# Query stage of a four-layer token kernel: where two routed blocks are located, and the order inside GpSimd's inverse root

## The reference, cut to what matters

```python
q_p = elu(einsum('bhnd,hdf->bhnf', q, proj)) + 1.0
attn = einsum('bhnf,bhfd->bhnd', q_p, kv) * z
x = x + attn.reshape(b, n, d) @ W_out.T + b_out
xt = layernorm(x)
logits = xt @ w_g                      # 8 experts, the top 2 are taken
exp_rank = cumsum(one_hot(top_i)) - 1  # a token's slot in its expert's list
exp_mask = exp_mask * (exp_rank < cap)
```

## Time and profile before

| what | us |
|---|---|
| median of 3 runs | 519.93 |
| the runs | 519.93, 519.01, 523.59 |
| the profiled execution's own time | 518.94 |
| its span | 517.2 |

### The profile page before, as it was taken

The page is one execution under the profiler, slowest core; times in us unless marked ns, Lnnn a source line. Parts: engine busy times, 40 slices in busy tenths (PEclk is TensorE's granted clock), DMA queues, the critical chain, the costliest instruction groups (busy, mean ns, idle before and its releaser), DMA issues.

```text
span 517.2 us, 7944 instructions
## 1 busy us (share of the span) xinstructions
PE 447.1 (86%) x2774; PEld 312.4 (60%) x2774; DVE 295.3 (57%) x712; ACT 228.7 (44%) x351; POOL 257.3 (50%) x321
## 2 busy tenths in 40 slices
PE   7889797968578999999999999889776989999980
PEld 5534253425578788888876333335355977887860
DVE  5879789998230021424486999899775201221254
ACT  5758554433020333324047998877652113323220
POOL 5989575898535945455431000021715542555460
PEclk9989777879778999999999999999978799999995
DMA  5465742991198222125423443340101121221277
GB/s 133 144 227 162 253 136 89 333 270 39 42 285 264 74 74 60 53 77 190 150 59 94 101 102 95 89 160 1 38 15 37 42 88 35 60 81 54 63 226 210
DMA packets 50327, 60.87 MB, mean 118 GB/s; under 512 B 7152, under 2 KB 29296, under 8 KB 50288
## 3 DMA queue, kind: packets, MB, share of 16 engines
q1 hardware_dynamic: 42672, 47.50, 31.1%
q0 software_dynamic: 4608, 8.47, 5.0%
q10 hardware_dynamic: 3008, 4.40, 2.7%
HBM read 29.78 MB, written 25.31 MB: 107 GB/s over the span
## 4 chain that ended last, share of the span: by engine, by line
PE 36%; issue 20%; SPq 12%; DVE 4%; DMA 3%; another core or an unknown queue 2%; ACT 1%; POOLq 0%; POOL 0%; ACTq 0%; DVEq 0%
PE ps L1342 29%; SPq L391 11%; PE ps L1346 5%; PE ps L1498 2%; DMA last_got<-chosen_y 1%; DMA slots_x<-rows_x,put_at 1%; DMA xe<-slots_x 1%; DMA chosen_y<-ye,y_to 0%; DMA stk<-part 0%; ACT xnT L586 0%; DVE xeT L1177 0%; POOLq L81 0%; DVE otok L997 0%; DVE xn L1237 0%
## 5 line engine op out<-in xcount | busy, mean ns | idle before, releaser
L543 POOL DMA_INDIRECT chosen_y<-ye,y_to x80 | 79.1, 988 | 78.0 <-DVE ye L1212 54.1
L493 POOL DMA_INDIRECT slots_x<-rows_x,put_at x64 | 62.7, 980 | 48.8 <-DVE put_at L1071 31.6
L1346 PE MATMUL ps<-ident 128*128 128x128 f32 x584 | 78.8, 298 | 6.4 <-DMA slots_x<-rows_x,put_at 3.2
L719 ACT ACTIVATE hT<-ps 128x640 f32<-128x640 f32 x64 | 45.1, 704 | 87.2 <-issue 49.5
L1346 PEld LDWEIGHTS ps<-ident 128*128 128x128 f32 x584 | 74.2, 156 | 9.1 <-DMA slots_x<-rows_x,put_at 3.9
L1266 DVE SCALAR_TENSOR_TENSOR feat<-expo,ps 128x1024 f32<-128x1024 f32 x64 | 76.4, 1217 | 2.4 <-ACT expo L848 2.0
L848 ACT ACTIVATE expo<-ps,minus_one 128x1024 f32<-128x1024 f32 x64 | 70.4, 1116 | 12.8 <-PE ps L1342 8.9
L1342 PE MATMUL ps<-cproj_sb,hT 128*128 128x128 f32 x640 | 74.6, 275 | 0.3
L1342 PEld LDWEIGHTS ps<-cproj_sb,hT 128*128 128x128 f32 x640 | 73.0, 192 | 0.9 <-issue 0.6
L1342 PE MATMUL ps<-xeT,cfc_sb 128*128 128x320 f32 x256 | 71.7, 433 | 2.1 <-DVE xeT L1177 2.1
L1177 DVE COPY xeT<-ps 128x640 f32<-128x640 f32 x16 | 13.2, 825 | 94.5 <-PE ps L1342 47.3
(11 more groups left out here) (230 smaller groups left out, 612.9 us busy)
## 6 DMA issues: line engine op xcount, KB each, us to landing
chosen_y<-empty_rows SPq DMA_DIRECT2D x32, 256.0 KB
decay<-k_rows SPq DMA_DIRECT2D x30, 256.0 KB, 4.8
stk<-part SPq DMA_DIRECT2D x96, 64.0 KB, 2.0
slots_x<-empty_rows SPq DMA_DIRECT2D x16, 325.0 KB, 5.7
xe<-slots_x SPq DMA_DIRECT2D x16, 325.0 KB
cfc_sb<-in_L_ffn_c_fc SPq DMA_DIRECT2D x2, 2048.0 KB, 9.1
got<-chosen_y SPq DMA_DIRECT2D x8, 256.0 KB
got<-chosen_y ACTq DMA_DIRECT2D x8, 256.0 KB
```

Of the source, the lines that this page charges most:

```text
L493: pool.indirect_dma_start(out=slots_x[k], out_offset=bass.IndirectOffsetOnAxis(ap=put_at[:, c, kk, t:t + 1], axis=0), in_=rows_x[:, kk * N ...
L543: pool.indirect_dma_start(out=chosen_y[k], out_offset=bass.IndirectOffsetOnAxis(ap=y_to[:, b, i:i + 1], axis=0), in_=ye[:, b, i * D:(i + 1 ...
L719: act.activation(hT[:, b, f, :].rearrange("p (a n) -> p a n", a=2), ps[:, 2 + 2 * (f % 2):4 + 2 * (f % 2), 0:HALF], ACT.Gelu).then_inc(h_r ...
L1346: pe.transpose(ps[:, bank, 0:P], ident[:], ident[:])
```

## The change

The rank slots of blocks 0 and 1 come one unit earlier: block 0 is located in slot 25, between units 5 and 6 of block 2, and block 1 in slot 36, between units 5 and 6 of block 3. Unit 6 moves to slots 26 and 37. All the rest keeps its slot. In `inverse_root`, `half` is computed right after `var_eps`, and the negated mean right after that, straight into `shift`; both without a link. The number of instructions on each engine is the same.

```diff
 def unit_slot(c, u):
-    return 8 * c + u + max(0, c - 1) + 2 * max(0, c - 2) + (u > 4) * (c >= 1) + ((u > 3) + (u > 6)) * (c >= 2)
+    return 8 * c + u + max(0, c - 1) + 2 * max(0, c - 2) + (u > 4) * (c >= 1) + ((u > 3) + (u > 5)) * (c >= 2)
...
-RANK_AT = {unit_slot(c + 2, 6) + 1: c for c in range(NB - 2)}
+RANK_AT = {unit_slot(c + 2, 5) + 1: c for c in range(NB - 2)}
...
                 link_root(pool.tensor_scalar(var_eps[:], mv[:, tt, 1], EPS, None, ALU.add))
+                pool.tensor_scalar(half[:], var_eps[:], 0.5, None, ALU.mult)
+                pool.tensor_scalar(shift[:, tt], mv[:, tt, 0], -1.0, None, ALU.mult)
                 link_root(pool.tensor_scalar(guess[:].bitcast(I32), var_eps[:].bitcast(I32), -0.5, float(0x5F3759DF),
                                              ALU.mult, ALU.add))
-                link_root(pool.tensor_scalar(half[:], var_eps[:], 0.5, None, ALU.mult))
                 y = guess[:]
                 for it in range(3):
                     new = rstd[:, tt] if it == 2 else guess[:]
...
                     link_root(pool.tensor_tensor(new, y_sq[:], y, ALU.mult))
-                link_root(pool.tensor_scalar(half[:], mv[:, tt, 0], -1.0, None, ALU.mult))
-                pool.tensor_tensor(shift[:, tt], half[:], rstd[:, tt], ALU.mult).then_inc(root_ready, 1)
+                pool.tensor_tensor(shift[:, tt], shift[:, tt], rstd[:, tt], ALU.mult).then_inc(root_ready, 1)
```

## The result

| | median us | runs |
|---|---|---|
| before | 518.86 | 20, from 515.98 to 524.88 |
| changed | 522.43 | 20, from 517.96 to 523.96 |

The changed kernel takes 1.0068 of the time of before, with a 95% interval of 1.0048 to 1.0087: **3.5 us slower** (2.5 to 4.5). That is inside the range of the forecast (517.3 to 523.3) and inside its 1%, but the forecast had 0.4 us, and the rest needs a cause.

What follows compares the result with a forecast made beforehand. The prediction took DVE's last feature of the query stage as the bound. PE's order +0.4, block 2 0 and root 0 gave 518.94 + 0.4 = 519.3 for the profiled execution; the median forecast was 520.3 us, range 517.3 to 523.3.

Steps and rivals of the forecast that it cites:

- What bounds the kernel: Query stage: the end is set by when DVE finishes the last feature, unit (3,7), at 385.27; GpSimd isn't the bound.
- Rival 3: GpSimd's scatters are the bound after all and blocks come down 1.16 us earlier: 518.8 us; chance 0.04.
- more than a few tenths: Sign of being wrong: last feature to block 3's first scatter, 26.1 us before, changes by more, meaning clock, not order.
- All that this buys is GpSimd's idle time: Block 1's numbers and scatters come 1.16 us earlier, only lengthening GpSimd's idle time before block 2: worth nothing.
- Rival 2: A second stall, or the clock, at product (3,6) behind the rank: slower, 524.3 us for 5.1 us of stall; chance 0.07.
- what I couldn't explain in full: One DMA queue carries code, 22 transfers, 0.36 MB; who asked for them or whether they delay anyone was unknown.
- rival 1: The stall of 370 to 378 goes away or shrinks, all of it 5.1 us: 514.8 us; chance 0.04 for most.
- those tenths: Block 0's scatters start 0.3 us earlier beside the stall of 370 to 378; otherwise nothing between 364 and 376 is touched.
- The run-ahead of PE: Block 3: product (3,6) issues behind rank and idle transposes, so the last feature is 0.4 us later; bounds 0 and 1.0.
- Block 2's part: Product (2,6) also issues behind the idle transposes, but its delay is hidden by 0.2 us: 0, at most +0.3.
- The root: Inverse root: two links fewer shorten its chain by about 0.26 us, worth nothing because ACT takes the result later.
- `ln_rows` of block 0 unmoved: Sign of being right: ACT's `ln_rows` of block 0 stays where it was despite the shorter root chain.

Runs made afterwards that it cites:

- block1_only: Kernel before with only block 1 located behind unit 5 (slot 36), block 0 and root as before: 522.73 us, ratio 1.0078.
- hold0_before: Kernel before, with block 0's eight scatters waiting for the residual of block 2 and block 1's following right behind: 524.47 us, ratio 1.0119.
- hold1_before: Kernel before, with block 1's eight scatters waiting until PE has made the router logits of block 2: 531.03 us, ratio 1.0204.
- the repeat: The changed kernel run once more, unaltered, against the kernel before at 520.99 us: 522.94 us, ratio 1.0059.
- slots_only: Kernel before with the rank slots of blocks 0 and 1 moved, the root as before: 522.29 us, ratio 1.0059.
- hold1_after: Changed kernel, with GpSimd holding back block 1's eight scatters until DVE has made the stage's last feature: 519.75 us, ratio 1.0010 against the kernel before.
- split0_again: Kernel before with block 0's scatters in two groups of four, run a second time, with the kernel before at 520.99 us: 524.34 us, ratio 1.0073.
- split0_before: Kernel before with block 0's scatters in two groups, the second four waiting for the feature of (3,4): 498.42 us, ratio 1.0017.

## Why the prediction was right or wrong

**What bounds the kernel** held: GpSimd is idle ahead of blocks 2 and 3 in every profile of the changed kernel (6.51 and 3.55 us), and an earlier location won nothing. Rival 3 is out. From the last feature's end to block 3's first scatter I had 26.1 us, and called more than a few tenths a sign that the clock had come in; it is 408.47 - 381.35 = 27.1 in the changed kernel and 414.79 - 386.29 = 28.5 in block1_only, and what was added are the waits at the pauses.

**"All that this buys is GpSimd's idle time" is the step that failed.** I asked what waits for the scatters, and never what runs beside them. Moved 1.16 us ahead of DVE's order, they made PE's results late at `turn_at`, the normalised rows and the logits of block 2 (in block1_only the waits for these are 3.53, 2.84 and 3.19 us, where before has 1.49, 0.42 and 1.68), and all three are on the chain that sets the end. The hold on GpSimd alone returned about 3 of 3.5 us in the medians.

**Rival 2** had the sign and the kind, a second pause behind (3,5), but the wrong place and cause: I looked for it between the rank and product (3,6), and priced it as a rare event (0.07). It comes behind the last feature, and in all five profiles of kernels with the early location and no hold. And as what I couldn't explain in full I listed the code transfers, and named the scatters beside the pause at 370 to 378 only in rival 1, with the effect of "those tenths".

The transfers of queue q8, of the kind "instruction" on the page, are 22 with 0.36 MB in the changed kernel too, and the pauses don't follow them. In hold0_before PE's program at 370 is the same and has no pause there (`choose` waits 0.38 us). And no transfer of that queue falls into the long pauses: the nearest are at 365 and 398 in hold0_before (pauses at 379 to 396) and at 394 and 424 in hold1_before (pause at 401 to 416), so none of them ended one.

**Rival 1** didn't come: DVE's two waits there were 2.20 and 1.99 us in the changed kernel's profile, where before had 3.04 and 2.15 (the 3.0 and 2.1 of its sum), but 4.37 and 0.80 in the repeat's.

**The run-ahead of PE** was right in its mechanism: the product of (3,6) late, a hole on DVE ahead of its feature, released by `expo`. Counted from `add_b` of block 2, the last feature ends 0.4 us later than before in slots_only and in the repeat of the changed kernel, 0.6 in block1_only, 0.7 in hold1_after and 1.2 in the changed kernel's own profile; I had 0.4 with bounds of 0 and 1.0. The idle transposes were sized too short (1.21 for 1.34 to 1.57). The half clock of its upper bound is in the trace of before, a granted clock of 0.50 from 378.0 to 380.9, and so is the full one of block 2, 1.00 from 357 to 361. Block 2's part was hidden, as said.

**The root** was worth nothing, as said. Its size was 0.16 us for 0.26: its operations without a link start 0.20 apart and not 0.15.

**The rest** of the text that checked out: `ln_rows` of block 0 unmoved relative to the stage (345.48 is 4.1 ahead, as all there), no change from block 0's location, and a range that the measured median fell into, near its upper end, 0.9 us below it. That was luck: the range was wide because of the spread of the runs, while the forecast of what the change costs, 0.2 to 1.0 us, missed the 2.5 to 4.5 that were measured.

## What to carry to other kernels

Ask of a transfer or a GpSimd instruction that is moved not only who waits for it, but which engines work while it runs: idle time of an engine off the chain isn't free room if its work slows another one. When a wait is released by "remote" or "issue" though the producer's record ended long before, line up the other engines' timelines against it, and move the suspect by one wait on its engine: here a single added wait told order from interference. And a profiled execution must be placed among the runs before its end is read: here the changed kernel's was the fastest of 20, and hold1_after's the slowest of 12.

## What the runs showed of the hardware that I had not expected

- Where the kernel before takes 519 to 521 us, PE's results came late while GpSimd sent indirect DMAs one behind the other (one each 1.28 us). Four in a row brought nothing (split0_again, 0.38 us of wait). With eight, DVE waited 3.04 us for block 1's logits and 2.15 ahead of `add_b` of block 2 (before), where hold0_before has 0.38 and no wait; and 3.10 us for block 2's logits (changed), where hold1_after has 1.58. Twelve brought 10.9 (split0_again), sixteen 7.6 + 8.1 and 14.6 us (hold0_before, hold1_before). The wait ends about when the group does: 415.97 behind a last start at 412.52 (hold1_before), 396.63 behind one at 393.14 (hold0_before). The instructions behind these waits are no longer than in before: `den` 0.19 and `eight` 0.39 us on DVE, `xnT` 0.60 on ACT.
- It isn't there always: where the kernel before takes 497.5 us, split0_before has none, with twelve scatters in a row (0.38 to 2.72 us of wait at the logits, 1.42 at the turned heads). What differs is open, and so is by what path the scatters reach PE: their work on GpSimd, the transfers that they start, or the signals.
- The granted clock was low behind the first long pause: in hold0_before PE was busy 3.84 of 9 us in it (378 to 387, granted clock still 0.96), and in the next 9 us, 387 to 396, the granted clock is 0.50, where before has 0.81 at these times. First hold0_before, then before:

```profile
387.00:396.00 9.00, 2.82 (x12) 2.42 (x12) 1.03 (x4) 1.12 (x2) 5.59 (x6) 0.50 0.16 52
```

```profile
387.00:396.00 9.00, 7.12 (x55) 6.11 (x54) 3.28 (x18) 3.38 (x8) 5.86 (x7) 0.81 0.17 54
```
